# A four-layer graph network on one core: TensorE's order at three joins, and GpSimd's adjacency loads issued at the head of each step

## The reference

```python
# layer 0: attention of scores h h^T masked by adj
node_att = softmax(x @ node_w, axis=0); h = x @ edge_w
e = where(adj > 0, h @ h.T, NEG_BIG)
out = adj * (node_att * softmax(e, axis=1)) @ (x @ weight) + bias
# layer 1: edge weights from two scores per node, and a gated sum
h = x @ W_sa; scores = (h @ a_l)[:, None] + (h @ a_r)[None, :]
e = where(adj != 0, exp(-leaky_relu(scores, 0.01)), 0)
x_a = (e / (e.sum(1) + 1e-5)) @ h
x_b = adj @ (x @ W_gcnb) + b_gcnb
out = sigmoid(attn_a * x_a + attn_b * x_b)   # attn_*: sigmoids of (adj @ x, x)
# layer 2: normalised adjacency with a diagonal added
out = relu(adj_norm @ (x @ weight))          # adj_norm = D^-1/2 (adj + I) D^-1/2
# layer 3: three graph convolutions
h = relu(adj @ (x @ W1) + b1); h = relu(adj @ (h @ W2) + b2); out = adj @ (h @ W3) + b3
```

## Time and profile before

| | us |
|---|---|
| median of 3 runs | 761.91 (761.52 to 769.05) |
| the profiled execution | 762.32 |
| its span | 760.5 |
| PE busy in the span | 733.7 (96%) |
| DVE / ACT / POOL busy | 430.3 / 345.2 / 126.3 |

### The profile page before, as it was taken

One profiled execution on the slowest core, in us unless ns is written; L12 is line 12 of the kernel. 1 busy time (PEld: TensorE's weight loads), 2 busy tenths in 40 slices (PEclk: granted clock), 3 DMA queues, 4 the chain that ended last, 5 costly groups with the idle time before them and its releaser, 6 DMA issues.

```text
span 760.5 us, 12140 instructions
## 1 busy us (share of the span) xinstructions
PE 733.7 (96%) x4663; PEld 536.7 (71%) x4707; DVE 430.3 (57%) x893; ACT 345.2 (45%) x529; POOL 126.3 (17%) x253
## 2 busy tenths in 40 slices
PE   6999899998999999999999999999999999999997
PEld 5878788897779686877755556575664646467886
DVE  3586888797597897978954484033180311214533
ACT  4688977794574555547521153142260412224000
POOL 2111422112400011202123320000001000000443
PEclk9999999999999999999999999999999999999999
DMA  6997799988469139000030000000000000000011
GB/s 186 202 149 162 167 184 161 169 146 160 89 105 177 26 73 151 14 1 1 1 92 0 1 1 1 0 1 0 1 3 27 0 1 0 0 0 1 29 43 42
DMA packets 112916, 48.82 MB, mean 64 GB/s; under 512 B 102561, under 2 KB 108321, under 8 KB 112865
## 3 DMA queue, kind: packets, MB, share of 16 engines
q1 hardware_dynamic: 108464, 32.65, 21.4%
q0 software_dynamic: 4400, 15.47, 11.8%
HBM read 35.53 MB, written 2.10 MB: 49 GB/s over the span
## 4 chain that ended last, share of the span: by engine, by line
PE 48%; DVE 5%; issue 2%; ACT 1%; POOL 0%; POOLq 0%; DVEq 0%; ACTq 0%
PE ps L830 13%; PE ps L984 11%; PE ps L959 8%; PE ps L1030 6%; PE ps L993 3%; PE ps L942 3%; PE ps L1019 2%; PE ps L669 1%; DVE es_lo L1358 1%; DVE x L1662 1%; DVE tm L1582 1%; PE ps L1009 1%; DVE stats L1370 1%; DVE y L1624 0%; DVE nb L1579 0%
## 5 line engine op out<-in xcount | busy, mean ns | idle before, releaser
L830 PE MATMUL ps<-adjT,x 128*128 128x512 bf16 x736 | 167.8, 379 | 3.3 <-DVE x L1662 1.4
L830 PEld LDWEIGHTS ps<-adjT,x 128*128 128x128 f16 x768 | 72.5, 98 | 85.6 <-issue 1.7
L1358 DVE TENSOR_TENSOR hh_lo<-hf,hh_hi 128x512 fp32r<-128x512 f32 x32 | 22.2, 692 | 134.0 <-ACT hf L1293 133.0
L749 PE MATMUL ps<-sup,turned 128*128 128x256 f16 x768 | 86.6, 273 | 1.2 <-DMA turned<-pl 1.2
L984 PE MATMUL ps<-adjT,G 128*128 x375 | 82.6, 379 | 0.9 <-ACT hf L1293 0.4
L749 PEld LDWEIGHTS ps<-sup,turned 128*128 128x128 f16 x768 | 74.2, 98 | 12.4 <-issue 3.8
L874 PE MATMUL ps<-H_hi,es_hi 128*128 128x258 f32 x256 | 76.8, 300 | 2.2 <-DVE es_lo L1358 1.7
L874 PE MATMUL ps<-H_hi,es_lo 128*128 128x258 f32 x256 | 72.4, 283 | 0.0
L874 PE MATMUL ps<-H_lo,es_hi 128*128 128x258 f32 x256 | 72.4, 283 | 0.0
L984 PEld LDWEIGHTS ps<-adjT,G 128*128 128x128 f16 x384 | 37.3, 98 | 45.4 <-issue 0.9
L508 POOL TENSOR_TENSOR rstd<-mv,epsc 128x1 f32<-128x1 f32 x64 | 16.5, 258 | 275.0 <-DVE mv L1372 274.9
(11 more groups left out here) (233 smaller groups left out, 1422.9 us busy)
## 6 DMA issues: line engine op xcount, KB each, us to landing
adjb<-in_adj POOLq DMA_DIRECT2D x14, 512.0 KB, 7.1
adjf<-in_adj POOLq DMA_DIRECT2D x14, 512.0 KB, 7.0
out<-adjf SPq DMA_DIRECT2D x16, 128.0 KB, 1.7
x<-in_x SPq DMA_DIRECT2D x3, 512.0 KB, 7.1
adjf<-in_L_gnn_W SPq DMA_DIRECT2D x1, 1024.0 KB, 6.1
x<-in_x SPq DMA_DIRECT2D x2, 256.0 KB, 3.0
W1f<-in_L_gnn_W SPq DMA_DIRECT2D x1, 512.0 KB, 3.3
adjf<-in_L_gnn_W SPq DMA_DIRECT2D x1, 512.0 KB, 3.6
```

Of the source, the lines that this page charges most:

```text
L749: ins = mm(bank(6 + u, D), PT(part, t)[:, jt, :], sup[:, jt, c0:c0 + D], start=(jt == 0 and (part, c0) == (HI, 0)), stop=(jt == T - 1 and ...
L830: ins = mm(bank(agg_bank(layer, b, f)), x16[:, 1 - part, jt, f * P:(f + 1) * P], adj(b, jt), start=(jt == 0 and part == HI), stop=(jt == T ...
L1358: return tt(to, frm, high.bitcast(F32), ALU.subtract)
```

## The change

On TensorE: the first pair of blocks 1, 2 and 3 of layer 1 goes through a new function `attend_first`, which does the 16 matmuls with the high edge weights first, waiting for `ef_ready` and the banks, and then the 8 with the low ones, waiting for `es_lo`. Block 0 of layer 2 does its last four tiles in `last_tiles`: the high part of each tile comes ahead of the low part of the tile before it. The last `out2` becomes `out2_last`: the piece f is the outer loop and the bank k the inner one. On GpSimd: `load_adj(t + 8)` stands ahead of `norm_factor(t)` and `bias_x(t + 2)` in its step.

```diff
--- before.py
+++ after.py
@@ -574,13 +574,13 @@
                 nc.gpsimd.tensor_scalar(x16[:, 1 - HI, t, :], x[:, t, :], XS, None, ALU.mult).then_inc(conv_hi, 1)
 
             for t in range(T):
+                if 2 <= t < T - 2 * AB:
+                    load_adj(t + 2 * AB)
                 norm_factor(t, t % 2)
                 if t + 2 < T:
                     bias_x(t + 2, t % 2, pv_read)
                 if t == 1:
                     load_weights()
-                if 2 <= t < T - 2 * AB:
-                    load_adj(t + 2 * AB)
                 if t in LATER_LOADED:
                     load_later(LATER_LOADED[t])
                 if t >= T - 3:
@@ -863,6 +863,19 @@
             agg_early(TURNS - 2, TURNS - 1)
             left_row(1)
 
+            def attend_first(b):
+
+                for low in (False, True):
+                    pe.wait_ge(es_lo if low else ef_ready, b * PAIRS + 1)
+                    for jt in (0, 1):
+                        for k in range(TB):
+                            if jt == 0 and not low:
+                                pe.wait_ge(z_ready, (b - 1) * TB + k + 1)
+                            for p, q in ((LO, HI),) if low else ((HI, HI), (HI, LO)):
+                                ins = mm(bank(k, D + 2), es[p][:, (b * T + jt) % RE, k * P:(k + 1) * P], H[q][:, jt, :],
+                                         start=(jt == 0 and (p, q) == (HI, HI)), stop=False)
+                ins.then_inc(e_used, 1)
+
             def attend(b, pair):
 
                 pe.wait_ge(es_lo, b * PAIRS + pair + 1)
@@ -900,7 +913,10 @@
                         left_row(3)
                         pe.wait_ge(H_ready, 2)
                         pe.wait_ge(p1_lo, T)
-                    attend(b, pair)
+                    if b and pair == 0:
+                        attend_first(b)
+                    else:
+                        attend(b, pair)
                     if pair == len(tiles) - 1:
                         if b == 0:
                             pe.wait_ge(sl_read, B)
@@ -919,16 +935,46 @@
                     pe.wait_ge(relu_ready, TB + (b - 1) * TB + k + 1)
                     project(bank(k, D), agg, slice(k * P, (k + 1) * P), wls, D).then_inc(o2_mm, 1)
 
+            def out2_last():
+
+                for f in range(KD):
+                    pe.wait_ge(agg_lo, (2 * B - 1) * KD + f + 1)
+                    for k in range(TB):
+                        if f == 0:
+                            pe.wait_ge(relu_ready, TB + (B - 2) * TB + k + 1)
+                        for p, q in ((HI, HI), (HI, LO), (LO, HI)):
+                            ins = mm(bank(k, D), agg[p][:, f, k * P:(k + 1) * P], wls[q][:, f, 0:D],
+                                     start=(f == 0 and (p, q) == (HI, HI)), stop=(f == KD - 1 and p == LO))
+                        if f == KD - 1:
+                            ins.then_inc(o2_mm, 1)
+
+            def last_tiles():
+
+                for jt in range(T - TB, T + 1):
+                    if jt < T:
+                        pe.wait_ge(conv_hi, T + jt + 1)
+                        for f in range(KD):
+                            mm(bank(agg_bank(1, 0, f)), x16[:, 1 - HI, jt, f * P:(f + 1) * P], adj(0, jt),
+                               start=False, stop=False)
+                    if jt > T - TB:
+                        pe.wait_ge(conv_lo, T + jt)
+                        for f in range(KD):
+                            ins = mm(bank(agg_bank(1, 0, f)), x16[:, 1 - LO, jt - 1, f * P:(f + 1) * P], adj(0, jt - 1),
+                                     start=False, stop=(jt == T))
+                            if jt == T:
+                                ins.then_inc(agg_mm, 1)
+
             pe.wait_ge(diag_added, TB)
-            for jt in range(T):
+            for jt in range(T - TB):
                 for f in range(KD):
                     aggregate_tiles(1, 0, f, (jt,))
+            last_tiles()
             for b in range(1, B):
                 pe.wait_ge(diag_added, TB * (b + 1))
                 aggregate(1, b, 0)
                 out2(b - 1)
                 aggregate(1, b, 1)
-            out2(B - 1)
+            out2_last()
             pe.drain().then_inc(l2_done, 1)
```

## The result

The changed kernel takes 770.37 us in the median (760.99 to 779.52, 22 runs), the kernel before 762.88 us in as many runs (761.01 to 780.22). By the medians that is 7.5 us or 1.0% slower. The forecast was 760.7 us and 0.2% faster. The slower rival, 766.7 us, is the one that came, for a reason close to the one it named, and larger.

A forecast was written before the change was run, and what follows sets the result against it. TensorE, busy 733.7 of 760.5 us, was taken as the bound, so only its standing still counts. Terms 0 + 0 + 0.8 + 0.36 = 1.2 us off 761.91 gave 760.7 us, 0.2% faster; range 758.9 to 763.6 us.

The forecast's parts named there:

- The slower rival: Earlier loads delay transposes, ScalarE or VectorE late to scores once a landing exceeds 10.6 us; 766.7 us, chance 0.07.
- Part 1: GpSimd's six loads issued 3 to 7 us earlier; transpose waits shift from ScalarE to VectorE, both covered; 0 gained.
- the value 0 taken from a range of 0 to 12 us: Moved loads' loss: six rounds, each past its cover by 0 to 2 us; taken as 0.
- 9.3 us as the worst landing: Longest landing of a transpose from 118 to 130 us, with loads about; the median there was 8.1 us.
- The row of 3.68 us: ScalarE's wait for a transpose of `ph` at 137.50 us, said to cost TensorE nothing; basis for taking no loss.
- the 1.3 us of cover: VectorE's second maximum ended at 141.4 us; TensorE needed it at about 142.7 us.
- the sum: The four parts' gains, 0 + 0 + 0.8 + 0.36 = 1.2 us off, giving 760.7 us, 0.2% faster.
- Part 2: `attend_first`, three times: no gain; pair 0 ends 0.38 us later, taken in by pair 1's wait; 0 taken.
- Its rival of 1.1 us: `attend_first` paid in full, pair 1's wait moving with pair 0: 1.1 us lost, 761.8 us, chance 0.15.
- Part 3: `last_tiles`: the whole stall before the low part of tile 13 goes, 0.8 us gained.
- Part 4: `out2_last`: bank 0 complete after three matmuls instead of six, so layer 3 starts earlier; 0.36 us gained.
- The rival in which layer 3's start does not move: Chain to weights' low parts hangs on something other than `relu2` of bank 0; only `last_tiles` pays: 761.1 us, chance 0.13.

The follow-up runs named there:

- e6: Changed kernel, each of the six loads also waiting until SyncE has issued the same round's transpose of `ph`: 760.02 us, 0.9963 of the kernel before.
- e3: Changed kernel, load still ahead of the norm factor but waiting for the same variance first: 775.11 us, 1.0125 of the kernel before.
- e9: e6 with `attend` in place of `attend_first`: 760.71 us, 0.9977 of the kernel before.
- e8: e6 with TensorE's order of before: 761.81 us, 0.9989 of the kernel before.
- e7: Changed kernel, loads waiting until SyncE has issued the transpose of `pl` of the round before: 763.77 us, 1.0003 of the kernel before.
- e5: TensorE's new order, GpSimd's old order, loads also waiting for SyncE's issue of `ph`'s transpose: 760.67 us, 0.9976 of the kernel before.
- e4: Changed kernel with the six moved loads cut to a quarter of their columns, output not the reference's: 760.25 us, 0.9959 of the kernel before.

## Why the prediction was right or wrong

**Part 1 is where it failed.** Right in it: the loads go out earlier (the first at 90.16 us, forecast 90.6; over the six by 1.6 to 6.1 us, forecast 3 to 7), nobody waits for the rows, the norm factors cost nothing (e6), and nothing is gained. Wrong is the step "I expect ScalarE's waits to shrink and some of VectorE's to appear, both covered", and with it the value 0 taken from a range of 0 to 12 us. ScalarE's waits hardly shrank (13.7 us in three waits, after 14.3 in eight), VectorE's grew from 2.9 to 10.0 us in two waits, and 3.1 us of them were not covered. Instead of the 0 the profiled execution shows 4.4 us (3.1 for VectorE's maxima, 0.4 given back at a transpose, 1.7 of clock). The median lost more, and how a slower execution of this kernel divides its loss is in no trace. Three things were missing.

The first is what makes a transpose slow. I priced a collision by overlap, the same from either side, and took 9.3 us as the worst landing. But the issues in SyncE's own timeline had a hint: the two transposes of `ph` behind a load took 5.51 and 3.76 us, the four ahead of it under 3. The kernel before had its loads 0.5 to 1.3 us behind `ph`'s transpose in four of six rounds, by the length of one norm factor and one bias, and so on the milder side (landings of 5.6 to 8.1 us). The row of 3.68 us that I used as "the worst place" came from one of the two rounds where the load was ahead, so it was not true that six rounds had borne such a collision: two had. Nor did any row show a transpose with one load ahead of it and the next one inside its issue, as the two that landed after 10.8 and 11.2 us had it.

The second is who waits. I worked out the 1.3 us of cover for ScalarE's wait and applied it to VectorE's. VectorE writes `pl` after a maximum and before the next, and is the fuller of the two there (39.35 us of 47, against 34.20); of its wait of 5.99 us, 2.65 reached TensorE, with the 2.7 us of weight parts in the same round. Without that work the maximum would have been done at about 133.44 + 1.14 = 134.6 us, when TensorE was just ending its matmuls (134.85 us). That is an estimate, and no run moved the work. The round of the small stop at 107 us holds 2.9 us of such work too (L1486 to L1489). So the cover was thinnest in these two rounds, and the 1.3 us that I read came from another one.

The third is the clock, which stands in no term of the sum. In the profiled execution it costs 1.7 us for 2.7 us of added waits. It goes with the time over the 22 runs: the mean granted clock is 0.998 and 0.999 in the two fastest and 0.989 to 0.994 in the three slowest. It is not all of it, since two runs of 768.93 and 769.18 us had 0.999 and 0.998.

The slower rival had the mechanism's place and its threshold (a landing of over 10.6 us; 10.8 and 11.2 were seen), but with 1 us a round and no clock it gave 766.7 us where the median is 770.4, and 0.07 was too small a chance. In favour of a larger one stood that the DMA engines were at 0.98, with no row about a load ahead of `pl`. The threshold fitted: the two landings beyond it belong to the two rounds in which TensorE stopped for a maximum behind a late transpose.

The rule cited from the Trainium skill (page "DMA: Bandwidth & Descriptors", section "Issuing engines are not separate DMA queues"), that transfers run on the same 16 engines and interleave whichever engine starts them, agrees with these traces but is not enough. The kernel before, e3 and e6 have the same transfers in these rounds and differ in when the loads are issued, and their slowest transposes from 93 to 150 us land after 9.3, 18.0 and 5.7 us.

**Part 2 held**: no gain, 0.38 us forecast per pair and 0.39 measured, all of it taken in by pair 1's wait (e9). Its rival of 1.1 us falls.

**Part 3 held in kind**: the stall is gone, 0.6 us against the 0.8 forecast.

**Part 4 held**: 0.5 us against 0.36, with TensorE standing still for 1.21 us before layer 3, as the prediction said (1.5). The rival in which layer 3's start does not move falls. The TensorE part is 1.1 us in the trace, 1.2 in the sum, 1.6 in e6 against e8, and 1.1 in e9 against e8.

## What to carry to other kernels

When a large transfer is moved, look at which small ones are issued just behind it on other queues, and at the engine that waits for each, not only at the total share; an order that only two engines' timing keeps can be worth a semaphore, as in e6, which is 0.37% faster than the kernel before and has 3 us of spread where the changed kernel has 18. Most of that 0.37% may be TensorE's new order: with the old one (e8) the semaphore's gain over the kernel before isn't clear of noise (0.9989), and what it surely brings is the narrow spread (3.2 us, where the kernel before beside it had 7.3). A stop of TensorE of 2 or 3 us can cost more than its length: a stop of 2.65 us was followed by 1.7 us of lost clock, one of 2.0 us by the same in two executions of eleven and by nothing in the others, and one of 2.65 us in e3 (ending at 143.47 us) by nothing. A profile of one execution is not enough to judge a kernel whose transfers race: read the spread of the runs first.

## What was not expected of the hardware

SyncE's issue of a DMA transpose took 1.6 us undisturbed and 2.5 to 6.6 us when a load of 512 KB by GpSimd had gone out 0.2 to 3.2 us before (before, after and e3). A load issued 0.2 to 1.3 us behind its start (before, e3 and e7) left the issue of `ph`'s transpose at 1.6 to 2.9 us, but not its landing: 5.6 to 15.6 us, where 3.8 to 5.4 us was usual with the load held back until the issue had ended (e5 and e6). A quarter of the bytes (e4) left no issue in these rounds over 3.13 us.

Why this is so is not shown. Nor is why three issues in e3 took 7.6 to 10.0 us, 5 to 8 us behind a load, nor the landing of 18.0 us there. The tie does not reach all: in e6 a transpose of `pl` 4.6 us behind a load took 3.65 us to issue, and one 4.0 us behind a later load (163.60 us, outside the six) 3.42 us; in the kernel before the latter took 4.58.
